# Folding two layer norms into neighbouring matmuls, splitting an inverse transform, and exponentiating one score bank ahead of its transposition

## The chip, the core and the metric

The kernel runs on one core of a Trainium2 chip. The metric is the device time of one execution in microseconds, less is better. The engines are named PE (TensorE, its weight loads shown as PEld), DVE (VectorE), ACT (ScalarE), POOL (GpSimd) and SP (SyncE, here a DMA queue).

## What is computed

One decoder layer on x of 16 x 64 x 128, with a layer norm ahead of each of three parts: self attention with 16 heads of 8 (whose reshape mixes positions and heads, so that a group of 64 rows attends to itself), an attention by circular correlation over FFTs, and a mixture of 8 experts of which each token takes 2.

```python
def _layernorm(x, axis=-1, eps=1e-05):
    m = jnp.mean(x, axis=axis, keepdims=True)
    v = jnp.var(x, axis=axis, keepdims=True)
    return (x - m) / jnp.sqrt(v + eps)
...
    x = x + _L0_attn_ref(_layernorm(x, axis=-1), L0_attn_Wqkv, ...)   # softmax(q k / sqrt(8)) v, then Wo
    x = x + _L0_xattn_ref(_layernorm(x, axis=-1), ctx_1024, ctx_1024, ...)
    x = x + _L0_ffn_ref(_layernorm(x, axis=-1), ...)
...
        corr = jnp.fft.irfft(jnp.fft.rfft(Q, axis=-1) * jnp.conj(jnp.fft.rfft(K, axis=-1)), n=Lv, axis=-1)
        top_vals, top_idx = jax.lax.top_k(corr, k_top)
        w = jax.nn.softmax(top_vals, axis=-1)
```

## The kernel before

The 1024 tokens are 8 tiles of 128, taken in 4 chunks of two tiles. Each piece of work is a step name.chunk.part, and `ORDER_TEXT` gives for every engine the order of its steps, written out in full; `BANK_TEXT` gives each PSUM result one of 8 banks. An engine takes its steps strictly in that order and waits in each for semaphores of the steps that it depends on, and PE also for the release of its bank by the step that held it last. There is no other scheduling, so a step that waits holds up all behind it on its engine.

Steps of a chunk, in order of dependence:

- Norm: st1 (statistics, DVE), rs1 (reciprocal deviation, two small operations on POOL, L308 and L310), nm1 (DVE, L467, two instructions: subtract the mean, multiply), xt (PE transposes xn, ACT copies it out).
- Attention: qkv (PE, then DVE adds the bias into `nat`, L481), vpar (POOL), ft (DVE, 32x32 transpositions, L492), vtr (PE and ACT), score (PE, L722, 32x64 pieces, into four banks of 128x512), then per bank smax (DVE, negated maximum of each head, L497), sub (DVE, adds it to the scores and writes one of three buffers of `low`, L503), pt (PE transposes `low`), exp (ACT, exponential out of PSUM into `prob`, L372); then pv (PE, L746; DVE normalises, L511 to L522), vt2, wo (PE; DVE adds to the residual `x12`, L528).
- Correlation: st2, rs2, nm2 (as above), dft (PE, forward transform of xn with the constant C_FWD), qp (PE; products with the keys' spectrum on DVE, L536 to L541), corr (PE, L785: three matmuls, each of 128 rows and 256 columns, into one bank), top (DVE, maxima and their places, L548 to L555), ex (ACT), w8 (DVE, six small parts), mix (POOL, L343), g, ov, y2 (PE, with copies on ACT; DVE adds y2 to `x12`). The context's transforms are cdft and cproj.
- Experts: st3, rs3, nm3, xt3, xtop (DVE, L597) and xsp (POOL) split the activation into two parts; gate and pick (DVE, eight small steps) choose the experts; wt (PE) turns the weights, SP stores them to DRAM and loads them back broadcast (wdma, L283 and L287) for rel. For each expert: up (PE, L834), rel (DVE, L641, scaled by the loaded weights), sq (ACT, L430), down (PE, L845, summed over experts); fin (DVE, L647) and store. up, rel, sq and down are numbered over the 32 pairs of chunk and expert. wtop, whi and wlo split the expert weights w_up (L602, L425, L328).

Each transposition or matmul in fp32 shows as two instructions in the trace. A warm-up of 12 matmuls opens PE's order. SP issues the loads; w_up (L278) is issued after all of x and the context have landed.

## Time and profile before

| | us |
|---|---|
| median of 3 runs | 143.54 (143.08 to 144.1) |
| the profiled execution's own time | 142.93 |
| its span from first to last instruction | 141.2 |
| PE busy | 123.0 (87%) |
| DVE busy | 104.1 (74%) |
| ACT busy | 54.9 (39%) |
| POOL busy | 38.5 (27%) |
| mean granted PE clock | 0.976 |

The span leaves 1.7 us of the profiled execution's time outside. Busy time is that of an engine's instructions; PE's are modelled at their ends. The shares are means over stages with different limits, so they are to be read by stretch.

### The profile page before, as it was taken

Reading aid. Unit: us, or ns where it says so; the run is one execution under the profiler, and the core shown is the slowest. Engines: PE = TensorE matmul, PEld = TensorE weight load, DVE = VectorE, ACT = ScalarE, POOL = GpSimd, SP = SyncE. Lnnn points to the kernel's source line nnn. Section 1 sums busy time; section 2 is a strip of 40 time slices with the busy share of each in tenths; the row PEclk is TensorE's granted clock in tenths of the full one; section 3 lists DMA queues with packets and bytes.
Section 4 is the critical chain, followed back from the end, with each engine's and each line's share of the span. In section 5 each row is a group of like instructions: output and inputs, shape, how many; then the busy total and the mean of one; then the engine's idle time right before and its main releaser. Section 6 shows DMA issues by size and latency. Waiting matters only on the chain.

```text
span 141.2 us, 4101 instructions
## 1 busy us (share of the span) xinstructions
PE 123.0 (87%) x1612; PEld 104.9 (74%) x1612; DVE 104.1 (74%) x341; ACT 54.9 (39%) x117; POOL 38.5 (27%) x71
## 2 busy tenths in 40 slices
PE   6749987856899998697899839999999999999992
PEld 2246556545788886585798836999989899999991
DVE  1349999999999879999797969836938664073711
ACT  2203354635517703172513034754325344170550
POOL 8579190460302020406663030411500300000000
PEclk9978999999999999999999986999999999999999
DMA  4888800000000000000000610610017172001001
GB/s 121 263 225 295 358 14 0 7 0 5 5 5 0 0 7 7 0 2 5 0 5 1 250 49 5 260 42 0 0 39 241 63 237 102 0 0 37 5 2 37
DMA packets 5027, 9.50 MB, mean 67 GB/s; under 512 B 368, under 2 KB 3856, under 8 KB 4240
## 3 DMA queue, kind: packets, MB, share of 16 engines
q1 hardware_dynamic: 4432, 8.50, 17.5%
q10 hardware_dynamic: 576, 0.73, 1.8%
q8 instruction: 13, 0.21, 0.6%
q14 instruction: 6, 0.05, 0.1%
HBM read 8.68 MB, written 0.56 MB: 65 GB/s over the span
## 4 chain that ended last, share of the span: by engine, by line
PE 51%; DVE 25%; issue 5%; DMA 4%; ACT 1%; POOL 1%; DVEq 0%
PE ps L845 21%; PE ps L834 14%; DVE negm L497 5%; DVE feat L492 4%; PE ps L785 4%; DVE low L503 3%; DMA wb_sb<-w_dram 3%; PE ps L821 2%; DVE nat L481 2%; DVE wtop L602 2%; PE ps L800 1%; DVE onat L511 1%; PE ps L792 1%; DVE topi L555 1%; PE ps L731 1%
## 5 line engine op out<-in xcount | busy, mean ns | idle before, releaser
L641 DVE SCALAR_TENSOR_TENSOR rel<-ps,wb_sb 128x512 f32<-128x512 f32 x32 | 21.8, 690 | 13.1 <-PE ps L834 7.2
L845 PE MATMUL ps<-wdn_sb,hid 128*128 128x128 f32 x256 | 30.6, 276 | 0.0
L430 ACT ACTIVATE hid<-rel 128x512 f32<-128x512 f32 x32 | 20.2, 631 | 25.1 <-DVE rel L641 16.9
L845 PEld LDWEIGHTS ps<-wdn_sb,hid 128*128 128x128 f32 x256 | 29.5, 192 | 0.3 <-issue 0.2
L834 PE MATMUL ps<-xhi,whi 128*128 128x256 f32 x64 | 19.2, 300 | 0.1
L834 PE MATMUL ps<-xhi,wlo 128*128 128x256 f32 x64 | 17.8, 278 | 0.0
L834 PE MATMUL ps<-xlo,whi 128*128 128x256 f32 x64 | 17.8, 278 | 0.0
L372 ACT ACTIVATE prob<-ps 128x512 f32<-128x512 f32 x16 | 9.1, 599 | 9.4 <-PE ps L731 9.4
L343 POOL TENSOR_TENSOR mix<-w,con 128x128 f32<-128x128 f32 x16 | 6.1, 412 | 23.3 <-DVE w L585 23.3
L834 PEld LDWEIGHTS ps<-xhi,whi 128*128 128x128 f32 x64 | 12.1, 189 | 0.5 <-issue 0.4
L834 PEld LDWEIGHTS ps<-xlo,whi 128*128 128x128 f32 x64 | 12.1, 189 | 0.0
L834 PEld LDWEIGHTS ps<-xhi,wlo 128*128 128x128 f32 x64 | 12.0, 188 | 0.0
L731 PE MATMUL ps<-con,low 128*128 128x128 f32 x64 | 9.3, 279 | 1.2 <-DVE low L503 1.1
L497 DVE TENSOR_REDUCE negm<-ps 128x8 f32<-128x512 f32 x16 | 10.3, 669 | 0.0
L503 DVE TENSOR_TENSOR low<-ps,negm 128x512 f32<-128x512 f32 x16 | 10.2, 673 | 0.0
L492 DVE STREAM_TRANSPOSE feat<-nat 128x512 f32<-128x512 f32 x16 | 10.0, 675 | 0.0
L785 PE MATMUL ps<-con,prod 128*128 128x256 f32 x24 | 7.0, 437 | 3.3 <-DVE rel L641 2.6
L722 PEld LDWEIGHTS ps<-feat 32*64 32x64 f32 x512 | 6.3, 130 | 4.7 <-issue 4.7
L722 PE MATMUL ps<-feat 32*64 32x64 f32 x512 | 7.3, 231 | 2.6 <-issue 1.5
L321 POOL TENSOR_TENSOR nat<-nat,con 128x256 f32<-128x256 f32 x8 | 5.1, 659 | 15.2 <-DVE nat L481 15.2
L310 POOL TENSOR_TENSOR rstd<-rstd,con 128x2 f32<-128x2 f32 x12 | 8.9, 745 | 1.0
L731 PEld LDWEIGHTS ps<-con,low 128*128 128x128 f32 x64 | 7.0, 141 | 3.0 <-DVE low L503 2.6
(103 smaller groups left out, 211.3 us busy)
## 6 DMA issues: line engine op xcount, KB each, us to landing
wb_sb<-w_dram SPq DMA_DIRECT2D x4, 1024.0 KB, 4.7
wup_sb<-w_up SPq DMA_DIRECT2D x1, 1024.0 KB, 6.0
wdn_sb<-w_down SPq DMA_DIRECT2D x1, 1024.0 KB, 8.0
c_sb<-ctxt SPq DMA_DIRECT2D x2, 256.0 KB, 6.8
out<-x_sb SPq DMA_DIRECT2D x4, 128.0 KB, 1.8
con<-consts SPq DMA_DIRECT2D x1, 400.0 KB, 3.0
wmid_sb<-w_mid ACTq DMA_DIRECT2D x1, 324.0 KB, 5.8
row_sb<-rows ACTq DMA_DIRECT2D x1, 260.0 KB, 4.9
```

Source lines behind the costliest of these rows:

```text
L310: nc.gpsimd.tensor_tensor(rstd[:, k, :], rstd[:, k, :], con[:, C_POW:C_POW + 2], ALU.pow).then_inc(done[name], 1)
L372: nc.scalar.activation(prob[:, a % 2, part].rearrange("p i t s -> p (i t s)"), psum("pt", a, part), ACT.Exp, scale=SCALE).then_inc(done["p ...
L430: nc.scalar.activation(hid[:, a % 3, :], rel[:, a % 2, :], ACT.Square).then_inc(done["sq"], 1)
L492: last = nc.vector.transpose(feat[:, c, a % 2, t].rearrange("p h (j r) -> p j h r", j=J), nat[:, t, c, :, :])
L497: nc.vector.tensor_reduce(negm[:, a, part, :], s_ps, AX.X, ALU.max, negate=True).then_inc(smax_ready, 1)
L503: nc.vector.tensor_tensor(low[:, step % 3].rearrange("p (h s) -> p h s", s=S), psum("score", a, part).rearrange("p (h s) -> p h s", s=S), ...
L641: nc.vector.scalar_tensor_tensor(rel[:, a % 2, :].rearrange("p (c t) -> p c t", c=2), psum("up", a).rearrange("p (c t) -> p c t", c=2), 0. ...
L722: last = mm(quads[r][S * g:S * (g + 1), S * h:S * (h + 1)], feat[32 * r:32 * r + 32, 0, a % 2, g, h, :], feat[32 * r:32 * r + 32, 1, a % 2 ...
L731: last = tr(t_ps[:, P * i:P * (i + 1)], low[:, step % 3, P * i:P * (i + 1)], ident)
L785: last = mm(c_ps[:, 0:NB * L], prod[:, a % 2, i, :], con[:, C_INV + NB * L * i:C_INV + NB * L * (i + 1)], start=(i == 0), stop=(i == 2))
L834: last = mm(z_ps[:, 2 * P * half:2 * P * (half + 1)], w[:, e, P * half:P * (half + 1)], r[:, c % 2, :], start=(i == 0), stop=(i == 2))
L845: last = mm(acc_ps[:, D * t:D * (t + 1)], hid[:, a % 3, 2 * P * half + P * t:2 * P * half + P * (t + 1)], wdn_sb[:, e, half, :], start=(e ...
```

## The change

- The norm ahead of qkv is folded. xt transposes raw x. The mean goes by centring the weights once: cent.0.0 (PE multiplies w_qkv by a matrix of 1/128, DVE subtracts the result from w_qkv) and cent.0.1 for the query weights of the second norm. The deviation goes into qkv's addition on DVE, now a scale and an add in one instruction. nm1 is gone.
- The norm ahead of dft is folded. dft reads `x12`; its deviation comes by fw: ACT scales the transform constant by it, two activations of 128 elements per chunk. nm2 is gone. `xn` shrinks to 4 tiles.
- The last of four score banks has no sub. DVE scales its negated maxima (negs, 128 x 8), and ACT takes exp(scale x score - maximum) out of the score bank head by head, 8 activations of 64 elements with a bias pointer (early), into a buffer of its own. PE transposes that, and ACT copies it to `prob` where it took exponentials. `low` has two buffers.
- corr is done in two halves: six matmuls of 64 rows and 128 columns, the two halves in different row halves of the array and in two banks.
- All orders but SP's and all banks are laid out anew.

The core of the diff; of the order texts, those lines that the text below speaks of.

```diff
     "PE": """
...
-        score.3.1 pt.2.3 vtr.3.1 pv.2.0 dft.1.0 pv.2.1 qp.1.0 pt.3.0 corr.1.0 g.0.0 pt.3.1 pt.3.2 pt.3.3 ov.0.0 pv.3.0 y2.0.0
-        vt2.2.0 pv.3.1 wo.2.0 g.1.0 ov.1.0 xt3.0.0 vt2.3.0 y2.1.0 gate.0.0 dft.2.0 wo.3.0 up.0.0 qp.2.0 up.1.0 up.2.0 xt3.1.0
-        up.3.0 corr.2.0 wt.0.0 dft.3.0 gate.1.0 up.4.0 qp.3.0 up.5.0 up.6.0 up.7.0 corr.3.0 wt.1.0 g.2.0 down.0.0 down.1.0
...
+        warm.12.0 xt.0.0 cent.0.0 cent.0.1 xt.1.0 qkv.0.0 qkv.0.1 xt.2.0 cdft.0.0 cdft.1.0 qkv.1.0 cproj.0.0 qkv.1.1 vtr.0.0
...
+        score.3.0 pt.2.3 score.3.1 vtr.3.1 pv.2.0 dft.1.0 pv.2.1 qp.1.0 pt.3.0 g.0.0 pt.3.1 corr.1.0 ov.0.0 pt.3.2 pt.3.3 y2.0.0
+        vt2.2.0 pv.3.0 pv.3.1 wo.2.0 xt3.0.0 vt2.3.0 gate.0.0 wo.3.0 g.1.0 dft.2.0 up.0.0 wt.0.0 qp.2.0 ov.1.0 dft.3.0 up.1.0
+        y2.1.0 qp.3.0 corr.2.0 up.2.0 up.3.0 corr.3.0 up.4.0 up.5.0 up.6.0 xt3.1.0 up.7.0 gate.1.0 g.2.0 down.0.0 ov.2.0 up.8.0
...
     "DVE": """
-        st1.0.0 nm1.0.0 st1.1.0 st1.2.0 nm1.1.0 st1.3.0 qkv.0.0 nm1.2.0 qkv.0.1 nm1.3.0 ft.0.0 ft.0.1 qkv.1.0 qkv.1.1 wtop.0.0
-        wtop.0.1 ft.1.0 ft.1.1 smax.0.0 smax.0.1 smax.0.2 sub.0.0 smax.0.3 sub.0.1 sub.0.2 sub.0.3 qkv.2.0 qkv.2.1 wtop.0.2
-        wtop.0.3 ft.2.0 ft.2.1 smax.1.0 smax.1.1 smax.1.2 smax.1.3 sub.1.0 sub.1.1 sub.1.2 pv.0.0 sub.1.3 pv.0.1 qkv.3.0 pv.0.2
-        qkv.3.1 ft.3.0 smax.2.0 smax.2.1 wo.0.0 smax.2.2 st2.0.0 smax.2.3 pv.1.0 sub.2.0 pv.1.1 nm2.0.0 pv.1.2 sub.2.1 sub.2.2
...
-        w8.1.3 w8.1.4 w8.1.5 y2.0.0 st3.0.0 pv.3.0 wo.2.0 pv.3.1 st2.2.0 nm3.0.0 pv.3.2 nm2.2.0 xtop.0.0 y2.1.0 st3.1.0 pick.0.0
-        wo.3.0 pick.0.1 st2.3.0 pick.0.2 nm3.1.0 pick.0.3 qp.2.0 pick.0.4 nm2.3.0 xtop.1.0 pick.0.5 pick.0.6 pick.0.7 top.2.0
-        top.2.1 pick.1.0 w8.2.0 pick.1.1 pick.1.2 w8.2.1 qp.3.0 w8.2.2 pick.1.3 w8.2.3 pick.1.4 w8.2.4 pick.1.5 w8.2.5 pick.1.6
-        pick.1.7 rel.0.0 rel.1.0 rel.2.0 rel.3.0 rel.4.0 top.3.0 top.3.1 w8.3.0 w8.3.1 w8.3.2 w8.3.3 w8.3.4 rel.5.0 w8.3.5
...
+        st1.0.0 cent.0.0 st1.1.0 cent.0.1 st1.2.0 qkv.0.0 st1.3.0 qkv.0.1 ft.0.0 ft.0.1 qkv.1.0 qkv.1.1 wtop.0.0 wtop.0.1 ft.1.0
+        ft.1.1 smax.0.0 smax.0.1 sub.0.0 sub.0.1 smax.0.2 smax.0.3 sub.0.2 negs.0.0 qkv.2.0 qkv.2.1 wtop.0.2 wtop.0.3 ft.2.0
+        ft.2.1 smax.1.0 smax.1.1 sub.1.0 pv.0.0 sub.1.1 pv.0.1 smax.1.2 pv.0.2 sub.1.2 smax.1.3 qkv.3.0 negs.1.0 ft.3.0 wo.0.0
...
+        top.0.0 wo.1.0 top.0.1 st2.1.0 w8.0.0 w8.0.1 w8.0.2 smax.3.0 w8.0.3 smax.3.1 w8.0.4 smax.3.2 w8.0.5 smax.3.3 sub.3.0
+        negs.3.0 sub.3.1 qp.1.0 sub.3.2 pv.2.0 top.1.0 pv.2.1 top.1.1 pv.2.2 w8.1.0 y2.0.0 w8.1.1 st3.0.0 w8.1.2 w8.1.3 pv.3.0
+        w8.1.4 pv.3.1 w8.1.5 nm3.0.0 pv.3.2 wo.2.0 st2.2.0 xtop.0.0 pick.0.0 pick.0.1 pick.0.2 wo.3.0 pick.0.3 st2.3.0 pick.0.4
+        pick.0.5 pick.0.6 pick.0.7 qp.2.0 y2.1.0 qp.3.0 top.2.0 st3.1.0 top.2.1 top.3.0 w8.2.0 top.3.1 w8.2.1 nm3.1.0 w8.2.2
+        w8.2.3 w8.2.4 w8.2.5 w8.3.0 w8.3.1 rel.0.0 w8.3.2 rel.1.0 w8.3.3 xtop.1.0 rel.2.0 w8.3.4 rel.3.0 w8.3.5 pick.1.0 rel.4.0
...
     "ACT": """
...
+        xt.0.0 xt.1.0 xt.2.0 cdft.0.0 cdft.1.0 cproj.0.0 vtr.0.0 whi.0.0 whi.0.1 vtr.0.1 vtr.1.0 cdft.2.0 vtr.1.1 xt.3.0 exp.0.0
+        cproj.1.0 exp.0.1 early.0.0 whi.0.2 whi.0.3 exp.0.2 exp.0.3 vtr.2.0 vtr.2.1 exp.1.0 vt2.0.0 exp.1.1 early.1.0 exp.1.2
+        exp.1.3 cproj.2.0 fw.0.0 vtr.3.0 exp.2.0 cdft.3.0 dft.0.0 exp.2.1 cproj.3.0 exp.2.2 vt2.1.0 early.2.0 ex.0.0 exp.2.3
+        vtr.3.1 fw.1.0 dft.1.0 early.3.0 g.0.0 exp.3.0 exp.3.1 ov.0.0 exp.3.2 exp.3.3 ex.1.0 vt2.2.0 xt3.0.0 vt2.3.0 gate.0.0
+        fw.2.0 g.1.0 dft.2.0 fw.3.0 wt.0.0 ov.1.0 dft.3.0 ex.2.0 ex.3.0 xt3.1.0 sq.0.0 sq.1.0 gate.1.0 g.2.0 sq.2.0 sq.3.0
...
     "POOL": """
...
-        vpar.2.0 vpar.2.1 wlo.0.2 wlo.0.3 vpar.3.0 vpar.3.1 rs2.0.0 rs2.1.0 mix.0.0 mix.1.0 rs3.0.0 rs2.2.0 xsp.0.0 rs3.1.0
-        rs2.3.0 xsp.1.0 mix.2.0 mix.3.0 rs3.2.0 xsp.2.0 rs3.3.0 xsp.3.0""",
+        rs1.0.0 x12.0.0 x12.1.0 rs1.1.0 x12.2.0 rs1.2.0 vpar.0.0 vpar.0.1 x12.3.0 rs1.3.0 vpar.1.0 vpar.1.1 wlo.0.0 wlo.0.1
+        vpar.2.0 vpar.2.1 wlo.0.2 wlo.0.3 vpar.3.0 rs2.0.0 vpar.3.1 rs2.1.0 mix.0.0 rs3.0.0 mix.1.0 rs2.2.0 xsp.0.0 rs2.3.0
+        rs3.1.0 mix.2.0 xsp.1.0 mix.3.0 rs3.2.0 xsp.2.0 rs3.3.0 xsp.3.0""",
...
+    if name == "corr":
+        return [(name, a, 0), (name, a, 1)]
...
-        xn = sb("xn", [P, TILES, D])
+        xn = sb("xn", [P, 4, D])
+        mean_of = sb("mean_of", [P, P])
+        fw = sb("fw", [P, 2, 2, 2 * 2 * NF])
...
-        low = sb("low", [P, 3, GROUPS * S])
+        low = sb("low", [P, 2, GROUPS * S])
+        early = sb("early", [P, GROUPS * S])
+        negs = sb("negs", [P, CHUNKS, GROUPS])
...
+                if name == "fw":
+                    act.wait_ge(done["rs2"], a + 1)
+                    if a == 0:
+                        act.wait_ge(ld_con, 16)
+                    if a >= 2:
+                        act.wait_ge(full["dft"], a - 1)
+                    for t in range(2):
+                        last = nc.scalar.activation(fw[:, a % 2, t], con[:, C_FWD:C_FWD + 2 * 2 * NF], ACT.Identity,
+                                                    scale=rstd[:, CHUNKS + a, t:t + 1])
+                    last.then_inc(fw_ready, 1)
...
+                if name == "early":
+                    act.wait_ge(negs_ready, a + 1)
+                    if a:
+                        act.wait_ge(turned, a)
+                    for h in range(GROUPS):
+                        last = nc.scalar.activation(early[:, S * h:S * (h + 1)], psum("score", a, QUAD - 1)[:, S * h:S * (h + 1)],
+                                                    ACT.Exp, bias=negs[:, a, h:h + 1], scale=SCALE)
+                    last.then_inc(early_ready, 1)
                 if name == "exp":
-                    act.wait_ge(full["pt"], QUAD * a + part + 1)
+                    if part == QUAD - 1:
+                        act.wait_ge(turned, a + 1)
+                    else:
+                        act.wait_ge(full["pt"], (QUAD - 1) * a + part + 1)
                     if a >= 2:
                         act.wait_ge(full["pv"], a - 1)
-                    nc.scalar.activation(prob[:, a % 2, part].rearrange("p i t s -> p (i t s)"), psum("pt", a, part), ACT.Exp,
-                                         scale=SCALE).then_inc(done["pt"], 1)
+                    if part == QUAD - 1:
+                        nc.scalar.copy(prob[:, a % 2, part].rearrange("p i t s -> p (i t s)"), psum("pt", a, part)).then_inc(done["pt"], 1)
+                    else:
+                        nc.scalar.activation(prob[:, a % 2, part].rearrange("p i t s -> p (i t s)"), psum("pt", a, part), ACT.Exp,
+                                             scale=SCALE).then_inc(done["pt"], 1)
...
+            nc.vector.memset(mean_of[:], 1.0 / D).then_inc(mean_ready, 1)
...
-                if name in ("nm1", "nm2", "nm3"):
-                    src = x_sb if name == "nm1" else x12
-                    k = CHUNKS * (int(name[2]) - 1) + a
-                    dve.wait_ge(stats_ready, LN_AT[("rs" + name[2], a)])
-                    dve.wait_ge(done["rs" + name[2]], a + 1)
-                    if name == "nm2":
-                        dve.wait_ge(full["xt"], a + 1)
-                    if name == "nm3":
-                        dve.wait_ge(full["dft"], a + 1)
-                    for t in range(2):
-                        last = nc.vector.tensor_scalar(xn[:, 2 * a + t, :], src[:, 2 * a + t, :], mv[:, k, t, 0:1], rstd[:, k, t:t + 1],
-                                                       ALU.subtract, ALU.mult)
+                if name == "nm3":
+                    k = 2 * CHUNKS + a
+                    dve.wait_ge(stats_ready, LN_AT[("rs3", a)])
+                    dve.wait_ge(done["rs3"], a + 1)
+                    if a >= 2:
+                        dve.wait_ge(full["xt3"], a - 1)
+                    for t in range(2):
+                        last = nc.vector.tensor_scalar(xn[:, 2 * (a % 2) + t, :], x12[:, 2 * a + t, :], mv[:, k, t, 0:1],
+                                                       rstd[:, k, t:t + 1], ALU.subtract, ALU.mult)
                     last.then_inc(done[name], 1)
+                if name == "cent":
+                    dve.wait_ge(full["cent"], part + 1)
+                    w = wmid_sb[:, W_Q:W_Q + D] if part else wqkv_sb[:]
+                    nc.vector.tensor_tensor(w, w, psum(name, 0, part)[:, 0:(D if part else 3 * D)], ALU.subtract).then_inc(done[name], 1)
...
+                    dve.wait_ge(done["rs1"], a + 1)
...
-                    nc.vector.tensor_tensor(nat[:, t, :, :, 32 - HD:32].rearrange("p c j d -> p (c j) d"), proj, bias,
-                                            ALU.add).then_inc(done["qkv"], 1)
+                    nc.vector.scalar_tensor_tensor(nat[:, t, :, :, 32 - HD:32].rearrange("p c j d -> p (c j) d"), proj,
+                                                   rstd[:, a, t:t + 1], bias, ALU.mult, ALU.add).then_inc(done["qkv"], 1)
...
+                if name == "negs":
+                    dve.wait_ge(smax_ready, QUAD * (a + 1))
+                    nc.vector.tensor_scalar(negs[:, a], negm[:, a, QUAD - 1], SCALE, None, ALU.mult).then_inc(negs_ready, 1)
                 if name == "sub":
-                    step = QUAD * a + part
-                    dve.wait_ge(smax_ready, step + 1)
-                    if step >= 3:
-                        dve.wait_ge(full["pt"], step - 2)
-                    nc.vector.tensor_tensor(low[:, step % 3].rearrange("p (h s) -> p h s", s=S),
+                    step = (QUAD - 1) * a + part
+                    dve.wait_ge(smax_ready, QUAD * a + part + 1)
+                    if step >= 2:
+                        dve.wait_ge(full["pt"], step - 1)
+                    nc.vector.tensor_tensor(low[:, step % 2].rearrange("p (h s) -> p h s", s=S),
                                             psum("score", a, part).rearrange("p (h s) -> p h s", s=S),
...
-                    corr = psum("corr", a)[:, 0:NB * L].rearrange("p (b s) -> p b s", s=L)
+                    corr = [psum("corr", a, b // 2)[:, L * (b % 2):L * (b % 2 + 1)] for b in range(NB)]
...
-                    dve.wait_ge(done["nm2"], a + 1)
+                    dve.wait_ge(full["dft"], a + 1)
...
-                    pe.wait_ge(low_ready, QUAD * a + part + 1)
+                    if part == QUAD - 1:
+                        pe.wait_ge(early_ready, a + 1)
+                    else:
+                        pe.wait_ge(low_ready, (QUAD - 1) * a + part + 1)
...
+                if name == "cent":
+                    if part == 0:
+                        pe.wait_ge(mean_ready, 1)
+                    pe.wait_ge(ld_mid if part else ld_wqkv, 16)
+                    w = wmid_sb[:, W_Q:W_Q + D] if part else wqkv_sb[:]
+                    mm(bank(name, 0, part)[:, 0:(D if part else 3 * D)], mean_of[:], w, start=True, stop=True).then_inc(full[name], 1)
                 if name in ("xt", "xt3"):
-                    if name == "xt" and a == 0:
-                        pe.wait_ge(ld_id, 16)
-                    pe.wait_ge(done["nm1" if name == "xt" else "nm3"], a + 1)
+                    if name == "xt":
+                        if a == 0:
+                            pe.wait_ge(ld_id, 16)
+                        pe.wait_ge((ld_x0, ld_x1, ld_x, ld_x)[a], 16)
+                    else:
+                        pe.wait_ge(done["nm3"], a + 1)
...
-                        last = tr(t_ps[:, P * t:P * (t + 1)], xn[:, 2 * a + t, :], ident)
+                        last = tr(t_ps[:, P * t:P * (t + 1)], x_sb[:, 2 * a + t, :] if name == "xt" else xn[:, 2 * (a % 2) + t, :], ident)
...
-                        pe.wait_ge(ld_wqkv, 16)
+                        pe.wait_ge(done["cent"], 1)
...
-                    step = QUAD * a + part
-                    pe.wait_ge(low_ready, step + 1)
+                    step = (QUAD - 1) * a + part
+                    if part == QUAD - 1:
+                        pe.wait_ge(early_ready, a + 1)
+                    else:
+                        pe.wait_ge(low_ready, step + 1)
                     t_ps = bank(name, a, part)
+                    source = early if part == QUAD - 1 else low[:, step % 2]
                     for i in range(PAIRS):
-                        last = tr(t_ps[:, P * i:P * (i + 1)], low[:, step % 3, P * i:P * (i + 1)], ident)
-                    last.then_inc(full[name], 1)
+                        last = tr(t_ps[:, P * i:P * (i + 1)], source[:, P * i:P * (i + 1)], ident)
+                    last.then_inc(turned if part == QUAD - 1 else full[name], 1)
...
-                    pe.wait_ge(done["nm2"], a + 1)
+                    pe.wait_ge(done["wo"], a + 1)
+                    pe.wait_ge(fw_ready, a + 1)
                     t_ps = bank(name, a)
                     spec = t_ps[:, 0:2 * P].rearrange("p (i t f) -> p i t f", i=2, t=2)
                     for t in range(2):
-                        last = mm(spec[:, :, t, :], xn[:, 2 * a + t, :],
-                                  con[:, C_FWD:C_FWD + 2 * 2 * NF].rearrange("p (i f) -> p i f", i=2), start=True, stop=True)
+                        last = mm(spec[:, :, t, :], x12[:, 2 * a + t, :], fw[:, a % 2, t].rearrange("p (i f) -> p i f", i=2),
+                                  start=True, stop=True)
...
+                    if a == 0:
+                        pe.wait_ge(done["cent"], 2)
...
-                    c_ps = bank(name, a)
+                    halves = [bank(name, a, two) for two in range(2)]
                     for i in range(3):
-                        last = mm(c_ps[:, 0:NB * L], prod[:, a % 2, i, :], con[:, C_INV + NB * L * i:C_INV + NB * L * (i + 1)],
-                                  start=(i == 0), stop=(i == 2))
+                        for two in range(2):
+                            rows = slice(2 * NF * two, 2 * NF * (two + 1))
+                            at = C_INV + NB * L * i + 2 * L * two
+                            last = mm(halves[two][:, 0:2 * L], prod[rows, a % 2, i, :], con[rows, at:at + 2 * L], start=(i == 0),
+                                      stop=(i == 2))
```

## Rows read from the trace of the kernel before

**Rows 1.** Windows of 10 us: window, length, busy time of each engine, clock, DMA.
```profile
10.00:20.00 10.00, 9.47 (x161) 6.17 (x159) 9.93 (x25) 4.33 (x8) 6.83 (x11) 0.90 0.67 249
...
20.00:30.00 10.00, 7.49 (x161) 5.66 (x162) 10.00 (x18) 5.44 (x10) 4.67 (x6) 1.00 0.01 2
...
40.00:50.00 10.00, 9.86 (x162) 8.74 (x161) 8.98 (x25) 6.07 (x14) 0.93 (x2) 1.00 0.02 4
...
60.00:70.00 10.00, 8.35 (x142) 6.92 (x140) 9.07 (x46) 5.30 (x18) 4.02 (x9) 1.00 0.01 2
...
80.00:90.00 10.00, 7.37 (x45) 5.68 (x44) 8.19 (x37) 4.09 (x8) 1.50 (x4) 0.83 0.22 88
...
100.00:110.00 10.00, 10.00 (x89) 9.62 (x88) 6.98 (x32) 3.94 (x8) 1.15 (x3) 1.00 0.34 116
```

**Rows 2.** Chain of work that ended last: start, length in us, what ran.
```profile
53.59 0.51 DVE xn L467 x2
...
74.58 1.29 PE ps L785 x6
...
78.16 4.24 DMA wb_sb<-w_dram
...
82.50 0.70 DVE rel L641
...
83.34 2.59 PE ps L785 x6
...
85.93 0.95 PE ps L821 x4
...
87.58 3.57 PE ps L845 x32
...
138.48 0.42 DVE x_sb L647
```

**Rows 3.** Timeline, four places: start, length, engine, line and operation.
```profile
10.37 0.34 SPq L278 DMA_DIRECT2D wup_sb<-w_up  x1
...
17.62 1.34 DVE L602 TENSOR_SCALAR wtop<-wup_sb 128x512 uint32<-128x512 uint32 x2
...
69.30 0.29 DVE L597 TENSOR_SCALAR xtop<-xn3T 128x256 uint32<-128x256 uint32 x1
...
70.84 0.36 PE L834 MATMUL ps<-xhi,whi 128*128 128x256 f32 x1
```

**Rows 4.** The page's DMA issues, w_up: count, size, us from issue to landing.
```profile
wup_sb<-w_up SPq DMA_DIRECT2D x1, 1024.0 KB, 6.0
```

**Rows 5.** Lines view, DVE: count, busy us, mean ns, idle before and releasers.
```profile
L503 DVE TENSOR_TENSOR low<-ps,negm 128x512 f32<-128x512 f32 x16 | 10.2, 673 | 0.0
...
L467 DVE TENSOR_SCALAR xn<-x,mv,rstd 128x128 f32<-128x128 f32 x16 | 4.7, 336 | 1.9 <-issue 1.9
...
L467 DVE TENSOR_SCALAR xn<-x_sb,mv,rstd 128x128 f32<-128x128 f32 x8 | 3.2, 443 | 1.2 <-POOL rstd L310 1.2
...
L560 DVE TENSOR_SCALAR topr<-topi 128x32 uint32<-128x32 uint32 x4 | 0.7, 164 | 0.0
...
L641 DVE SCALAR_TENSOR_TENSOR rel<-ps,wb_sb 128x512 f32<-128x512 f32 x32 | 21.8, 690 | 13.1 <-PE ps L834 7.2 <-ACT hid L430 4.4 <-DMA wb_sb<-w_dram 1.0
```

**Rows 6.** Lines view, ACT and POOL.
```profile
L385 ACT COPY valsT<-ps 128x64 f32<-128x64 f32 x16 | 2.2, 232 | 1.1 <-PE ps L754 1.0
...
L372 ACT ACTIVATE prob<-ps 128x512 f32<-128x512 f32 x16 | 9.1, 599 | 9.4 <-PE ps L731 9.4
...
L310 POOL TENSOR_TENSOR rstd<-rstd,con 128x2 f32<-128x2 f32 x12 | 8.9, 745 | 1.0
```

**Rows 7.** PE with small tiles: two pieces of the chain, one of the lines view.
```profile
48.45 0.84 PE ps L722 x53
...
96.22 0.61 PE ps L800 x16
...
L746 PE MATMUL ps<-prob,vkey 128*32 128x64 f32 x256 | 5.4, 222 | 0.6 <-issue 0.6
```

82 lines of the change are left out of this document (39 added, 43 removed).

## Prediction

> **What bounds the kernel now.** I read the windows first. From 10 to 60 us VectorE (DVE) is busy for 9 to 10 us of every ten, while TensorE (PE) has 7.5 to 9.9; from 90 us on PE is full and DVE is at 6 us or less of most tens. The hand-over lies in between: 60 to 70 has both near full, and in 80 to 90 PE stands still for 2.6 us at a granted clock of 0.83 [rows 1]. Then the chain of waits, in order of time: it runs almost wholly over DVE up to 44 us and again from 51 to 64, and from 69 us on over PE, with one detour: the expert weights of chunk 0 are stored and loaded back, rel.0 starts at 82.50, PE resumes at 83.34, and its first down is at 87.58. From there PE runs without a break to 138.46, where the last addition starts [rows 2]. So there are two terms to ask for: when DVE gets to xtop.0 (69.30 us, the last DVE step before the first up, whose matmuls start at 70.84 [rows 3]), and how long PE takes from there.
>
> The order texts make this clean: up to xtop.0 both kernels give DVE the same steps, but for eight nm1, nm2 and sub.3 kinds that go and the cent and negs steps that come. The tally of the set is exact; only its order changes.
>
> **Step A, the start.** The four nm1 go: 8 instructions, 3.2 us busy [rows 5], partly in gaps. cent.0 and cent.1 come: a subtraction of 384 and one of 128 elements. The forward pass qkv no longer waits for a normalised tile; its scale is folded into the addition, now a three-operand form. The form of L641 costs 690 ns for 512 elements and the plain addition of L503 673 [rows 5], so I price that at nothing. DVE would reach the first wtop about 2 us sooner than 17.62, but that step reads w_up, issued at 10.37 by SP behind the same waits as before [rows 3] and landing 6.0 us later [rows 4], at 16.4. So the gain is 17.6 - 16.4 = 1.2 us. SP's queue is untouched. On PE cent.1 stands ahead of xt.1 and qkv.0 and waits for w_mid; what is queued there is hidden as long as it delays qkv.0 by less than the 0.8 us that DVE would otherwise wait for w_up; beyond that the 1.2 shrinks, to 0 at worst. I take 1.2.
>
> **Step B, DVE from the first wtop to xtop.0.** This stretch was 69.30 - 17.62 = 51.7 us. Removed: four sub.3 at 10.2/16 = 0.64 us, 2.5 us; three nm2 (nm2.3 lies behind) of two instructions each, which took 0.51 us on the chain [rows 2] (4.7/16 = 0.29 apiece by the lines [rows 5], less overlap), 1.5 us. Added: four negs of 32 bytes a partition, like L560 at 164 ns [rows 5]; each follows its last smax and may wait a tenth, so 0.7 to 1.0, taken as 0.8. Sum: -3.2 us. low has two buffers where it had three: sub now waits for the transposition two steps back; two smax or another step stand between in each chunk, 0.6 us or more against a group of four matmul pairs of the same size, so I take nothing.
>
> **Step C, what ScalarE (ACT) takes over.** early: 8 activations of 64 elements from PSUM per chunk, 32 in all. The nearest row is L385, copies of 64 elements from PSUM: 232 ns each alone, 2.2/16 = 0.14 when overlapped [rows 6]. So one early is 1.1 to 1.9 us; I take 1.9, where a sub took 0.64. fw: two activations of 128 elements a chunk, 0.3 to 0.6 us. ACT is busy 6.1 us of the densest ten [rows 1], so this is load that fits; latency counts. The tightest chunk is 1: after negs.1 DVE has six passes over 512 elements a partition (two in ft.3.0, three smax, a sub) at L503's 0.64, and wo.0 and st2.0, some 1.2 together, so 5.0 us till it wants pv.1. Against that stand early 1.9, the transposition 0.5, exp.2 and the copy at 0.6 each [rows 6] and the pv matmuls, 5.4/4 = 1.35 less overlap [rows 7]: 4.6 to 5.0. So 0 to 0.4 us of cover; I add 0.5 us for this and its like. The bounds: 0, and 4 x 0.8 = 3.2 if all chunks are that tight and nothing overlaps.
>
> ScalarE has, by the Trainium skill's page "ScalarE: Activation LUTs", section "What ACT_TABLE_LOAD costs", 280 ns + 0.833 ns per element for an activation whose bias is a per-partition pointer, with some 93 ns overlapped: an estimate of 333 - 93 = 240 ns each, 1.9 us an early. L385 has no such pointer, so no run here shows it yet; it would leave the sum as it is.
>
> **Step D, from xtop.0 to the first down.** Before: 87.58 - 69.30 = 18.3 us, of which rel.0 starts at 82.50 - 69.30 = 13.2, with 1.0 of waiting for the wb load [rows 2, 5]. After, pick.0 is done first, so wt.0 comes early and the load (4.24 us for the way back alone [rows 2]) is off the path. In the DVE queue before rel.0, pick.1, xtop.1 and nm2.3 (13 instructions) are replaced by top.3 and the first of w8.3 (12), like for like: 12.2 us. But new waits appear. st2.2 now stands right before xtop.0, so on POOL rs2.2 (0.75 us [rows 6] and a small operation ahead of it, some 1.0) runs ahead of xsp.0, and dft.2, ahead of up.0 on PE, needs rs2.2 and then fw.2: up.0 starts 2.4 us after xtop.0, not 1.5. wt.0 then waits for the picks until 3.6. Behind it PE has qp.2 (result at 4.7; DVE is free at 3.4, idle 1.3), then ov.1, dft.3, up.1, y2.1 (result at 6.9; DVE free at 6.0, idle 0.9). So rel.0 starts at 12.2 + 2.2 = 14.4. g.2 and the first down follow rel.1, whose bank g.2 takes: 0.7 + 0.2 + 0.7 + 0.1 + a g of 0.5, at 16.7. Before, this took 5.1 us, since corr.3, wt.1 and g.2 came then at half clock (2.59 and 0.95 against 1.29 for the same corr [rows 2]). PE idles as long as before (xt3.1 waits for nm3.1, gate.1 for rel.0, some 3 us), but in pieces; I take full clock. D = 16.7 - 18.3 = -1.6 us.
>
> **The corr in halves** lies in this stretch for chunks 2 and 3. Before, 6 instructions take 1.29 us, 215 ns each. After, 12 of half the rows and half the columns. If pairs run side by side, 12 x 107/2 = 0.65; if not, 1.3. L722, 32-row pieces of 64 columns, goes at 0.84/64 = 13 ns each (the row counts 53 of a part's 64, some records are missing), where a full-height one of that width would take 54; L800, side by side in columns, at 0.61/16 = 38 [rows 7]. By the first 0.65, by the second 0.91; I take 0.8, with its entry and exit. That saves 0.5 a chunk. It is 2.0 us of PE over four chunks, but most goes into PE's idle time in this stretch; I count none beyond D.
>
> A rule speaks against it: the Trainium skill's "TensorEngine Tiling (Array Packing)", section "Key Properties", has TensorE drain on a change of tiling mode. In the chain L800's 16 pieces follow and precede full-height ones within 0.1 us [rows 7]; by the rule with a full drain at both ends the saving of 0.5 would be near nothing, by the row it stays.
>
> **Step E, behind the first down.** 138.46 - 87.58 = 50.9 us of unbroken PE. wt.1 now lies in it (+0.45); nothing else is added or removed. DVE and ACT have cover (PE 10.00, DVE 7 or less [rows 1]).
>
> **Sum.** -1.2 - 3.2 + 0.5 - 1.6 + 0.45 = -5.05 us: span 141.2 to 136.15. The profiled execution took 142.93, so 137.9; the median of the runs is 0.6 above it, 143.54, so 138.5.
>
> **Rivals.**
> Both waits go (0.13): DVE loses nothing in C and finds qp.2 and y2.1 ready, and PE's idle time before the first down falls away. -0.5 - 2.2 = 135.8, down to 134.5 with the corr saving in full. For it: the order was laid anew. Against: the queue positions above.
> Halves in series (0.10): corr stays at 1.3, 0.5 more for each of chunks 2 and 3: 139.5. L800 speaks for it, L722 against. By a rule of the skill's "TensorE: Matmul & The Clock Gate", section "LDWEIGHTS", a weight load goes by columns whatever its rows, so the halves load twice as much; the time it gives is this one.
> Given back at the hand-over (0.15): the waits of D double (+2.2) and PE's clock falls in them as at 83 us, (2.59 - 1.29) + 0.45 = 1.75 more: 142.5, no change. For it: PE stalls there in the kernel before too.
> Slower (0.10): early is slow on ACT, and DVE waits for pv in every chunk. It needs to eat 5.05 + 1.4 = 6.45 us, 1.6 a chunk; with cover 0.4, an early of 1.9 + 0.4 + 1.6 = 3.9 us, 0.49 per activation, twice L385. At 0.55 the time is 143.54 + 2 = 145.5.
>
> **How the numbers follow.** The forecast has 0.52 and its own range 137 to 140.5 (C from 0 to 1.5, A from 0.6 to 1.2). A measurement tells about 1% from no change, 1.4 us: faster is below 142.1. Faster: 0.52 + 0.13 + 0.10 and a little of the third rival, 0.77; same 0.13; slower 0.10. The range, leaving out the slower case, the top of the given-back one and the tail of the first rival, is 134.8 to 142.4.
>
> **What would show it.** Step A: first wtop (L602 before) at 16.4. B: xtop.0 at 65.4, DVE idle under 1 us between. C: 32 activations at about 0.23 in the lines view; ACT as releaser of DVE's pv if wrong. D: rel.0 14.4 and the first down 16.7 us behind xtop.0, granted clock 1.0 in between. Halves: 12 instructions in 0.8. E: 51.3 us of PE to the end. Most likely to be wrong: D, which hangs on queue positions rather than rows, and then C.

## The result, and the profile after

| | before | after |
|---|---|---|
| median of the runs, us | 143.74 (143.08 to 144.1) | 139.2 (137.75 to 139.81) |
| ratio to the kernel before | 1 | 0.9675, 95% interval 0.9586 to 0.9764 |
| profiled execution, its own time | 142.93 | 139.81 |
| its span, mean granted clock | 141.2, 0.976 | 138.0, 0.975 |

Ratios leave out runs over 1.5% above the shortest of the same kernel; medians are of all runs.

The change makes the kernel 3.2% faster, and 138.5 us had been forecast. Part of this agreement is luck. The prediction's sum gave the profiled execution a span of 136.15 us and a time of 137.9; they are 138.0 and 139.81, so 3.1 of the 5.05 us came. The median agrees because 0.6 us was added for a median above the profiled execution, and this time the profiled execution is the longest of four, 0.6 above the median. Inside the sum, terms were wrong in both directions: the start and VectorE's work shrank by more than counted, TensorE stood still in a place where nobody had looked, and the stretch behind the first down grew.

Line numbers of the kernel after: wtop L639, xtop L634, qkv L515, negs L534, sub L540, early L390, fw L374, score L773, pt L786, corr L846, up L895, wt L882, rel L678, down L906. The windows view, columns as in [rows 1]:

```profile
10.00:20.00 10.00, 9.37 (x178) 7.09 (x176) 9.93 (x23) 5.61 (x10) 8.15 (x12) 1.00 0.67 248
20.00:30.00 10.00, 6.81 (x155) 5.70 (x155) 9.81 (x18) 6.25 (x17) 4.01 (x4) 0.82 0.01 2
30.00:40.00 10.00, 9.05 (x224) 6.94 (x223) 6.22 (x14) 4.82 (x18) 0.61 (x1) 0.83 0.01 3
...
60.00:70.00 10.00, 6.99 (x106) 5.42 (x106) 8.41 (x44) 4.70 (x20) 5.46 (x12) 1.00 0.02 4
...
80.00:90.00 10.00, 9.24 (x84) 8.06 (x86) 8.90 (x33) 5.73 (x11) 4.91 (x12) 1.00 0.01 3
```

The kernel before had this between 30 and 40 us:

```profile
30.00:40.00 10.00, 7.89 (x255) 6.37 (x255) 10.00 (x20) 3.74 (x10) 1.89 (x3) 1.00 0.01 3
```

Against [rows 1], the hand-over (80 to 90) has lost its standstill and its low clock: PE 9.24 where it had 7.37. But between 20 and 40 us something new has come: the granted clock is 0.82 and 0.83, and in the second ten VectorE, the bound of this stretch, is busy only 6.22 us where it had 10.00. The timeline shows it, PE first, then the one DVE row with a long wait:

```profile
23.47 1.52 PE L773 MATMUL ps<-feat 32*64 32x64 f32 x121 [0.45 <-DVE low L540]
27.13 0.48 PE L773 MATMUL ps<-feat 32*64 32x64 f32 x7 [2.15 <-issue]
...
33.56 0.72 DVE L548 STREAM_TRANSPOSE onat<-ps 128x512 f32<-128x512 f32 x1 [3.75 <-PE ps L801]
```

Inside score.1.1 PE stops for 2.15 us, waiting for nothing that the profile shows, and the clock is at 0.50 (the 1.2 GHz level) from 27 to 33 us. The step pv.0 comes late and DVE stands 3.75 us. Then the hand-over and its end, the timeline again:

```profile
15.47 1.29 DVE L639 TENSOR_SCALAR wtop<-wup_sb 128x512 uint32<-128x512 uint32 x2
...
70.40 0.42 DVE L573 TENSOR_TENSOR prod<-ps,kv 128x256 f32<-128x256 f32 x1 [1.65 <-PE ps L833]
72.82 0.42 DVE L627 TENSOR_TENSOR x<-ps,x 128x256 f32<-128x256 f32 x1 [1.27 <-PE ps L868]
...
80.12 0.36 PE L895 MATMUL ps<-xhi,whi 128*128 128x256 f32 x1 [0.55 <-ACT xn3T L445]
81.44 0.58 PE L875 MATMUL ps<-wmid_sb,xn3T 128*128 128x8 f32 x4 [0.40 <-DVE rel L678]
82.84 1.13 PE L906 MATMUL ps<-wdn_sb,hid 128*128 128x128 f32 x8 [0.17 <-ACT eg L448]
```

xtop.0 starts at 65.77, rel.0 at 80.62 and the last addition at 135.36, so the 3.1 us by which that addition starts sooner are made of four parts:

| stretch | before | after | difference |
|---|---|---|---|
| to the first wtop | 17.62 | 15.47 | -2.15 |
| first wtop to xtop.0 | 51.68 | 50.30 | -1.38 |
| xtop.0 to first down | 18.28 | 17.07 | -1.21 |
| first down to the last addition | 50.90 | 52.52 | +1.62 |

The second row is what the experiments are about. Theory 1: it was to be -2.7 (B and C), and the standstill ate half of it. Theory 2: the early exponential on ScalarE is itself what makes pv.0 late. The two rivals of the prediction that the profile alone can't settle are also tested: what the halves of corr are worth, and where the hand-over's bound is.

### The profile page after: what moved, and what is told of

It reads as the page before. It is cut to its first block, busy times and chain, and to the rows that moved or that the text cites. A ratio compares the mean times of both kernels' runs of the same rounds, so it can differ in the third digit from the quotient of the medians.

```text
span 138.0 us, 4192 instructions
## 1 busy us (share of the span) xinstructions
PE 122.7 (89%) x1640; PEld 105.4 (76%) x1640; DVE 97.8 (71%) x328; ACT 63.9 (46%) x157; POOL 38.1 (28%) x71
## 4 chain that ended last, share of the span: by engine, by line
PE 53%; DVE 30%; issue 8%; DMA 5%; SPq 1%; ACT 0%; DVEq 0%
PE ps L906 20%; PE ps L895 14%; DMA x_sb<-x 5%; DVE feat L526 4%; DVE low L540 3%; DVE negm L531 3%; PE ps L801 3%; PE ps L786 3%; PE ps L773 2%; DVE rel L678 2%; DVE topi L592 2%; DVE nat L515 2%; PE ps L882 2%; DVE vals L557 1%; PE ps L743 1%
## 5 line engine op out<-in xcount | busy, mean ns | idle before, releaser
L678 DVE SCALAR_TENSOR_TENSOR rel<-ps,wb_sb 128x512 f32<-128x512 f32 x32 | 21.6, 684 | 13.9 <-ACT hid L461 9.8
L461 ACT ACTIVATE hid<-rel 128x512 f32<-128x512 f32 x32 | 20.2, 631 | 24.4 <-PE ps L906 14.0
L906 PE MATMUL ps<-wdn_sb,hid 128*128 128x128 f32 x256 | 31.0, 277 | 0.2 <-ACT eg L448 0.2
L906 PEld LDWEIGHTS ps<-wdn_sb,hid 128*128 128x128 f32 x256 | 29.5, 192 | 0.9 <-issue 0.8
L895 PE MATMUL ps<-xhi,whi 128*128 128x256 f32 x64 | 19.1, 298 | 0.7 <-ACT xn3T L445 0.6
L895 PE MATMUL ps<-xlo,whi 128*128 128x256 f32 x64 | 17.9, 279 | 0.0
L895 PE MATMUL ps<-xhi,wlo 128*128 128x256 f32 x64 | 17.9, 279 | 0.0
L895 PEld LDWEIGHTS ps<-xhi,whi 128*128 128x128 f32 x64 | 12.0, 188 | 1.5 <-issue 1.3
L895 PEld LDWEIGHTS ps<-xhi,wlo 128*128 128x128 f32 x64 | 12.0, 188 | 0.0
L895 PEld LDWEIGHTS ps<-xlo,whi 128*128 128x128 f32 x64 | 12.0, 188 | 0.0
L773 PE MATMUL ps<-feat 32*64 32x64 f32 x512 | 7.5, 232 | 3.4 <-issue 2.4
L773 PEld LDWEIGHTS ps<-feat 32*64 32x64 f32 x512 | 6.4, 131 | 5.1 <-issue 4.4
L315 POOL TENSOR_SCALAR rstd<-mv 128x2 f32<-128x2 f32 x12 | 2.7, 222 | 25.0 <-DVE mv L487 25.0
L403 ACT ACTIVATE prob<-ps 128x512 f32<-128x512 f32 x12 | 7.2, 615 | 3.7 <-PE ps L786 3.7
L786 PE MATMUL ps<-con,low 128*128 128x128 f32 x48 | 7.8, 290 | 0.8 <-DVE low L540 0.8
L540 DVE TENSOR_TENSOR low<-ps,negm 128x512 f32<-128x512 f32 x12 | 7.9, 665 | 0.0
L409 ACT COPY vkey<-ps 128x512 f32<-128x512 f32 x8 | 4.6, 586 | 6.3 <-PE ps L801 3.5
```

The source lines that it names most:

```text
L403: nc.scalar.activation(prob[:, a % 2, part].rearrange("p i t s -> p (i t s)"), psum("pt", a, part), ACT.Exp, scale=SCALE).then_inc(done["p ...
L461: nc.scalar.activation(hid[:, a % 3, :], rel[:, a % 2, :], ACT.Square).then_inc(done["sq"], 1)
L540: nc.vector.tensor_tensor(low[:, step % 2].rearrange("p (h s) -> p h s", s=S), psum("score", a, part).rearrange("p (h s) -> p h s", s=S), ...
L678: nc.vector.scalar_tensor_tensor(rel[:, a % 2, :].rearrange("p (c t) -> p c t", c=2), psum("up", a).rearrange("p (c t) -> p c t", c=2), 0. ...
L773: last = mm(quads[r][S * g:S * (g + 1), S * h:S * (h + 1)], feat[32 * r:32 * r + 32, 0, a % 2, g, h, :], feat[32 * r:32 * r + 32, 1, a % 2 ...
L786: last = tr(t_ps[:, P * i:P * (i + 1)], source[:, P * i:P * (i + 1)], ident)
```

## The experiments

All are compared with runs of the kernel before on the same chip. Those of each group also shared one chip: after_again, full_corr, sub_back and norm2_back; norm1_back, pt_first, fill and warm24; pt_first_again, rel_early, sub_pt and norm1_fair.

**The changed kernel once more**

> The changed kernel unaltered, as the yardstick for the partial ones on the same chip. Expected 139.2 us, some 0.97 of the kernel before. Its profile shows PE standing still for 2.15 us in the second score step (released by nothing the profile shows) and then half clock for about 7 us. If that belongs to the place in the instruction stream, it is there again at the same matmul; if it was an accident of one execution, it is gone or elsewhere.

139.6 us, ratio 0.9655 (0.9553 to 0.9757). The same place stalls again, for 1.88 us, and this time DVE waits 2.27 us for pv.0 and 0.78 for w_up at the first wtop:

```profile
16.52 0.76 DVE L639 TENSOR_SCALAR wtop<-wup_sb 128x512 uint32<-128x512 uint32 x2 [0.78 <-DMA wup_sb<-w_up]
...
27.38 0.34 PE L773 MATMUL ps<-feat 32*64 32x64 f32 x7 [1.88 <-issue]
```

So here w_up ends step A's gain, as predicted, 6.0 us after its issue. In the first execution it landed after 5.1 us, and DVE reached the first wtop at 15.47 without a wait.

**What the stall is: its place and what moves it**

Edits, against the changed kernel: in pt_first one PE step goes ahead of score.1.1; fill adds eight warm-up matmuls of 512 columns to that step; warm24 makes the warm-up of 24 matmuls of half the columns.

```diff
-        pt.0.1 score.1.0 score.1.1 pt.0.2 pt.0.3
+        pt.0.1 score.1.0 pt.0.2 score.1.1 pt.0.3
```

> One swap in PE's order: pt.0.2 goes ahead of score.1.1 (the second half of chunk 1's scores). Theory (the stall belongs to the place in PE's instruction stream, where new code is not there yet): it falls 4 matmuls earlier in score.1.1, after 57 to 59 of its 64 instead of 61, pt.0.2 and its exponential are no longer behind it, and the time falls by 0.3 to 1 us. Rival (the stall belongs to the score step itself): still before the last 3 to 7 pieces.

> As the swap above, and 8 matmuls of 512 columns on the warm-up's zeros, whose result is overwritten, stand in pt.0.2 before its transpositions. They take 1.7 us of PE where it would stand still. Theory: code arrives meanwhile, no stall or one of under 0.5 us is left in score.1.1, the granted clock stays at 1.0 from 27 to 34 us, DVE's idle time before pv.0 (3.75 us) is mostly gone, and the time falls by 1.5 to 3 us. Rival: the stall only moves behind the extra work and the time rises by up to 1.7 us.

> The warm-up has 24 matmuls of 256 columns instead of 12 of 512: same columns, 12 more matmuls in PE's stream. Theory of the place in the stream: the stall comes 12 matmuls earlier in score.1.1, after about 49 of 64. Rival (a time of its own, or the step itself): it stays before the last 3 to 7 pieces. Total time as the changed kernel's within 1 us.

PE's matmuls were counted from the start to the standstill, one window each. The kernel before:

```profile
0.00:29.90 29.90, 23.14 (x339) 14.70 (x340) 22.57 (x54) 11.43 (x20) 18.21 (x29) 0.94 0.47 151
```

The changed kernel, and then warm24:

```profile
0.00:26.50 26.50, 21.57 (x339) 14.14 (x340) 19.38 (x48) 12.85 (x28) 17.45 (x28) 1.00 0.55 171
```

```profile
0.00:26.50 26.50, 20.88 (x339) 15.44 (x340) 18.70 (x47) 12.64 (x28) 16.90 (x28) 1.00 0.54 171
```

339 matmuls in each, whichever steps those are (the same count in the other kernels with a stop, but 340 in norm1_back and norm1_fair). In pt_first the stop leaves 11 pieces of score.1.1 where 7 were left, 4 earlier, as the theory of the place had it (a transposition shows as one instruction, not two, so pt.0.2 counts 4); the expectation had only started from the wrong piece. Twelve more matmuls at the start make the stall come 12 pieces earlier (timeline of warm24: x109, then x19 after 2.19 us), and the kernel before has it too ("30.60 0.33 PE L722 ... x3 [1.46 <-issue]" in its timeline). So it is a place in PE's instruction stream, not a step. The DMA view says what comes shortly before: one packet of queue q8, of kind "instruction", 16 KB or a little more, here with a smaller one of q14 in the same slice (in the kernel before only that of q8 falls into such a window):

```profile
DMA  0000000000090000000000000000000000000000
GB/s 0 0 0 0 0 0 0 0 0 0 0 197 0 0 0 0 0 0 0 0 0 0 0 0 0 0 0 0 0 0 0 0 0 0 0 0 0 0 0 0
...
q8 instruction: 1, 0.02, 1.8%
q14 instruction: 1, 0.01, 0.5%
```

This is the window from 23 to 28 us in 40 slices, so the packet runs at 24.4 and PE goes on at 27.13, 2.7 us later. In the kernel before the packet is at 27.8 and PE goes on 2.8 later, in warm24 at 24.8 and 2.6 later, in norm1_back at 28.6 and 2.4 later, in rel_early at 25.1 and 2.2 later. In fill the packet is at 25.1. PE, held up by the eight long matmuls, reaches the place 45 pieces into score.1.1, at 27.6 or so, 2.5 us behind the packet, and runs through all 64 without a wait in the trace:

```profile
24.75 1.90 PE L786 MATMUL ps<-heat 128*128 128x512 bf16 x8
26.48 0.60 PE L788 MATMUL ps<-con,low 128*128 128x128 f32 x4
27.01 1.11 PE L772 MATMUL ps<-feat 32*64 32x64 f32 x64
```

The pieces of score take 12.6 ns each (1.52 us for 121), so the reading is that PE had used up the instructions it held before the next block could be used. It rests on the place, the time of the packet and fill; no run changed the supply itself. The Trainium skill's "Runtime: NRT & Kernel Launch", section "Instruction fetch mechanics", has instructions fetched in blocks of 16 KiB while the engine runs, mostly hidden; here they are not, by 1.0 to 2.2 us (0.98 in rel_early, 2.19 in warm24).

fill took 139.13 us (0.9683, 0.9599 to 0.9767) and pt_first 138.66 (0.9617, 0.9509 to 0.9725), their spans 136.1 and 136.0. That fill is no faster than pt_first, against the 1.5 to 3 us expected of it, doesn't price the stall: its long matmuls only fill the time that PE stands in pt_first, and the pieces of pv.0 start at 29.72 in the one and at 29.41 in the other. What the two share is pt.0.2 ahead of the place, so that ACT has exp.0.2 to do meanwhile and only pt.0.3 queues behind it; the clock stayed at 1.00 from 26 to 32 us in both. Both spans are 2 us shorter than the changed kernel's 138.0; in the medians less is left, 0.5 to 0.9 us for pt_first and 0.1 to 0.5 for fill. warm24, a single run, took 141.61 where the changed kernel's time within 1 us was expected, with 139.8 of span and clock 0.963.

**What the early exponential is worth**

Edit (sub_back): the fourth bank goes back to DVE and the common exponential; sub_pt is the same on top of pt_first.

```diff
-                    nc.vector.tensor_scalar(negs[:, a], negm[:, a, QUAD - 1], SCALE, None, ALU.mult).then_inc(negs_ready, 1)
+                    nc.vector.tensor_tensor(early[:].rearrange("p (h s) -> p h s", s=S),
+                                            psum("score", a, QUAD - 1).rearrange("p (h s) -> p h s", s=S),
+                                            negm[:, a, QUAD - 1, :].unsqueeze(2).broadcast_to([P, GROUPS, S]), ALU.add).then_inc(early_ready, 1)
```

> Undoes one part: the fourth score bank is again shifted on DVE, then turned, then exponentiated; the orders are kept, the subtraction stands where the scaling of the maxima (negs) stood. DVE gets 4 x (0.64 - 0.15) = 2.0 us more, ACT 7.0 us less. Theory: DVE is the limit up to xtop.0, so 2 us slower than the changed kernel. Rival: ACT's latency was costing what DVE gained, or DVE has idle time there (3.75 us in front of pv.0), so less than 0.7 us slower, or faster.

> The changed kernel with one step moved on PE: pt.0.2 from behind score.1.1 to ahead of it. It is the base of the two kernels run with it and is run again so that they can be set against it on one chip. Expected: 138.7 us as before (ratio to the kernel before 0.962); in the trace PE stands still 1.5 us inside score.1.1 after 53 of its 64 matmuls, no low clock from 27 to 34 us, xtop.0 at 63.1 us, first down at 80.8, and a second stretch of low clock at 63 to 67. If the low clock after the stall comes and goes from run to run, its times fall apart by about 2 us, between 137.7 and 139.8.

> The kernel pt_first_again with the early exponential taken back (sub.3 on DVE, four score banks treated alike). If moving the fourth bank to ACT is worth what the prediction gave it (DVE 2.5 us less, 0.8 for negs, 0.5 of waiting: 1.2 us), this one is 1.2 us slower than pt_first_again, once the stall that hid it in sub_back is out of the way: xtop.0 at 64.3 instead of 63.1. If it is worth nothing, because the eight short exponentials of one bank are as late for the transposition as sub.3 was, both are within 0.3 us. If the early exponential costs, xtop.0 comes before 63.0, as it did in sub_back (64.08 against 64.83).

sub_back: 140.16 us, 0.9782 (0.9689 to 0.9875), 0.6 above after_again, so its rival (less than 0.7) held and not the 2 us. pt_first_again: 138.37, 0.9668 (0.9618 to 0.9719). sub_pt: 139.55, 0.9727 (0.9672 to 0.9782), as expected. Four windows, each from the first wtop to xtop.0, columns as in [rows 1] (DVE's is the third busy time): the kernel before, the changed kernel, pt_first_again, sub_pt.

```profile
17.62:69.30 51.68, 42.92 (x999) 34.79 (x998) 49.55 (x146) 24.23 (x59) 16.08 (x26) 1.00 0.02 4
```

```profile
15.47:65.77 50.30, 41.66 (x935) 34.04 (x921) 45.94 (x140) 30.48 (x93) 14.79 (x24) 0.93 0.05 17
```

```profile
15.95:62.89 46.94, 38.79 (x898) 31.54 (x886) 45.84 (x138) 30.29 (x93) 14.25 (x23) 1.00 0.04 14
```

```profile
16.16:64.05 47.89, 39.38 (x922) 31.75 (x913) 47.55 (x138) 24.00 (x61) 14.38 (x24) 1.00 0.04 15
```

DVE's work falls by 3.6 us in both kernels with early (49.55 to 45.94 or 45.84); its idle time is 2.1 us before, 4.4 in the changed kernel and 1.1 with pt.0.2 moved. Early alone is the step from sub_pt to pt_first_again: 1.7 us less work, 0.28 us of new waiting for pv.0 and 0.36 for wo.0, and xtop.0 1.16 us sooner (0.95 counted from the first wtop); the medians are 1.2 apart, though the intervals overlap. In the order of the change that gain is not there: xtop.0 comes at 64.08 in sub_back and at 65.77 and 64.83 in the changed kernel. So neither the stall nor early costs much alone. In sub_back the same stall of 1.88 us is followed by no fall of the clock and no wait of DVE for pv.0. PE's steps behind the stall are the same in both, up to the pieces of pv.0 (first sub_back, then the changed kernel's pv.0):

```profile
27.33 0.34 PE L766 MATMUL ps<-feat 32*64 32x64 f32 x7 [1.88 <-issue]
...
29.71 1.10 PE L794 MATMUL ps<-prob,vkey 128*32 128x64 f32 x64
```

```profile
31.58 1.90 PE L801 MATMUL ps<-prob,vkey 128*32 128x64 f32 x64
```

From the end of the stall to the end of pv.0 that is 3.48 us at full clock, 6.35 in the changed kernel and 5.15 in after_again, in none of them with a wait of PE in between. An estimate from these rows: 2.9 of the 3.75 us that DVE waits, and 1.7 of the 2.27 in after_again, are the half clock; the remaining 0.6 to 0.9 is the stall, felt because DVE, with less work, comes to pv.0 sooner. PE did not wait there for early's result, ready at 25.3, so theory 2 holds only for the 0.28 and 0.36 us above. Whether early has a part in the fall of the clock stays open: sub_back is one trace.

**The halves of corr**

```diff
-                        for two in range(2):
-                            rows = slice(2 * NF * two, 2 * NF * (two + 1))
...
+                        last = mm(halves[0][:, 0:NB * L], prod[:, a % 2, i, :], con[:, C_INV + NB * L * i:C_INV + NB * L * (i + 1)],
+                                  start=(i == 0), stop=(i == 2))
```

> Undoes one part: corr again as three matmuls of 128 rows and 256 columns, in one bank, all else of the changed kernel kept. In the changed kernel the 12 halves took 0.87 to 0.89 us where the 6 full ones took 1.29, so 0.4 a chunk. Theory of the prediction (most of it goes into idle time of PE): within 0.5 us of the changed kernel. Rival (PE is the limit from chunk 0's corr on): 4 x 0.4 = 1.6 us slower.

141.91 us, 0.9878 (0.9788 to 0.9969); the span is 1.6 us longer than after_again's, the median 2.3, so the rival held. corr.0 starts 0.1 us later than in after_again, xtop.0 1.2 and the first down 1.6. The timelines, first of full_corr and then of the changed kernel:

```profile
48.46 0.63 DVE L585 MAX8 topv<-ps 128x8 f32<-128x64 f32 x4 [0.38 <-PE ps L843]
58.51 0.63 DVE L585 MAX8 topv<-ps 128x8 f32<-128x64 f32 x4 [0.45 <-PE ps L843]
...
74.00 1.46 PE L843 MATMUL ps<-con,prod 128*128 128x256 f32 x6
```

```profile
73.16 0.94 PE L846 MATMUL ps<-con,prod 64*128 64x128 f32 x12
```

Full corr takes 1.46 us a chunk, the halves 0.94. The prediction took 0.5 a chunk and counted none of it outside the hand-over. But in chunks 0 and 1 DVE waits for corr before its maxima, 0.38 and 0.45 us, and there are no such waits in after_again: a faster PE step is worth something in the stretch that DVE bounds, where DVE waits for that very step.

**Undoing the two folds**

> Undoes one part: nm2 is a DVE step again (two instructions a chunk, placed behind smax.2.2, smax.3.1, pick.0.2 and pick.0.7) and fw is gone from ACT. Theory: 3 to 4 x 0.51 us more on DVE, of which two lie ahead of xtop.0 and one delays wt.0: 1.0 to 1.5 us slower than the changed kernel. Rival: DVE's idle time at qp.2 and y2.1 takes it in: within 0.5 us.

142.25 us, 0.9824 (0.9731 to 0.9918), 2.7 above after_again where 1.0 to 1.5 were expected; its shortest run took 141.32. Its profile has 142.3 of span at a clock of 0.952, so it prices the fold only roughly. From the first wtop to xtop.0 it takes 50.82 us: 0.5 more than the changed kernel's first execution, whose stall (2.15) and wait for pv.0 (3.75 against 3.77) are alike, and 2.5 more than after_again, where 1.0 us was expected for two nm2.

> Undoes one part: nm1 is a DVE step again, xt transposes its result, the addition behind qkv is the plain one and the centring of w_qkv is gone; only the query weights are centred. Theory: DVE gets 8 instructions of 0.3 to 0.4 us in the first 14 us, so the first wtop starts some 2 us later (17.5 where the changed kernel had 15.47), and all behind it by as much: 1.5 to 2.1 us slower. Rival: the stall of PE in the second score step ends at a time of its own, so that the later start costs less than 0.7 us.

> The changed kernel with the first layer norm's fold undone (nm1 by DVE ahead of the transposition) and, unlike norm1_back, with the start of the kernel before: its order of nm1, st1 and qkv on DVE, cdft.0 ahead of qkv.0 on PE, and a place of its own for every nm1, so that nm1.3 waits for no transposition. Prediction step A: the fold is worth 1.2 us at the first wtop plus 1.9 less for qkv's scaling that comes back, so 1.2 to 2 us in all: 141.0. If norm1_back's 4.3 us were the fold's own worth, 143.5 here too. The first wtop tells: 17.6 us if the start of the kernel before is restored (norm1_back had 19.5). If PE standing from 6.4 to 8.3 brings the low clock of 8 to 12 us that the kernel before shows, PEclk reads 0.5 to 0.8 in that stretch again.

norm1_back: 143.84 us, 0.9943 (0.9885 to 1.0001). norm1_fair: 144.93, 0.9988 (0.9925 to 1.005). Their ratios lie 0.029 and 0.033 above after_again's, some 4 to 5 us, so both miss the 1.2 to 2.1 us expected, and neither measures the fold alone: the first wtop comes at 19.50 and 21.39, later than the 17.62 of the kernel before. POOL of norm1_back shows why, and DVE behind it:

```profile
13.30 0.61 POOL L328 TENSOR_TENSOR nat<-nat,con 128x256 f32<-128x256 f32 x1 [0.96 <-DVE nat L524]
13.88 0.73 POOL L321 TENSOR_TENSOR x<-x_sb,row_sb 128x256 f32<-128x256 f32 x1
14.57 0.22 POOL L315 TENSOR_SCALAR rstd<-mv 128x2 f32<-128x2 f32 x1
14.87 0.71 POOL L317 TENSOR_TENSOR rstd<-rstd,con 128x2 f32<-128x2 f32 x1
```

```profile
15.67 0.60 DVE L506 TENSOR_SCALAR xn<-x_sb,mv,rstd 128x128 f32<-128x128 f32 x2 [2.45 <-issue]
```

The change has put rs1.3 behind vpar.0 on POOL, which is harmless where the reciprocal deviation is wanted only after qkv. With nm1 back, DVE waits 2.45 us for it. norm1_fair, which mended PE's and DVE's order but not POOL's, has this wait too (2.46) and another of 3.19 for cent.1. Taking 2.45 off norm1_back's 19.50 gives 17.05, 0.5 to 1.6 us behind the changed kernel: what step A had. That is worked out, not measured, so what the first fold is worth stays open.

The same runs show a part of the fold that the prediction missed. The windows of 8 to 12 us, kernel before and then after:

```profile
8.00:10.00 2.00, 1.05 (x5) 1.08 (x6) 0.99 (x6) 0.00 (x0) 1.89 (x4) 0.64 0.74 174
10.00:12.00 2.00, 2.00 (x6) 1.37 (x5) 1.93 (x10) 0.59 (x1) 1.92 (x4) 0.50 0.81 228
```

```profile
8.00:10.00 2.00, 2.00 (x11) 1.42 (x12) 1.20 (x7) 0.37 (x1) 1.26 (x4) 1.00 0.79 178
10.00:12.00 2.00, 2.00 (x17) 1.74 (x16) 1.93 (x9) 1.44 (x3) 1.92 (x4) 1.00 1.00 255
```

Before, PE stands from 6.5 to 8.95 us and then works at half clock until 12. The fold gives it cent.0, cent.1 and a transposition of raw x in that gap, and the clock stays full. With nm1 back the low clock is back (0.64 and 0.50 in norm1_fair).

**The hand-over in another order**

Edit, on top of pt_first, DVE's order and then PE's, cut to the steps that move (on ACT gate.1 also goes ahead of sq.1):

```diff
-  top.3.0 w8.2.0 top.3.1 w8.2.1 nm3.1.0 w8.2.2 w8.2.3 w8.2.4 w8.2.5 w8.3.0 w8.3.1 rel.0.0 w8.3.2 rel.1.0
+  top.3.0 top.3.1 nm3.1.0 rel.0.0 w8.2.0 w8.2.1 w8.2.2 rel.1.0 w8.2.3 w8.2.4 w8.2.5 rel.2.0 w8.3.0 w8.3.1
...
-  gate.1.0 g.2.0 down.0.0 ov.2.0 up.8.0 down.1.0 g.3.0
+  gate.1.0 down.0.0 down.1.0 g.2.0 ov.2.0 up.8.0 g.3.0
```

> The kernel pt_first_again with the hand-over in another order: on DVE top.3.1, nm3.1 and rel.0 ahead of w8.2, on PE down.0 and down.1 ahead of g.2, on ACT gate.1 ahead of sq.1. Theory (the hand-over is held by DVE's order, as prediction step D has it: rel.0 is not late because the broadcast of the gates is late): rel.0 goes from 78.6 to 76.4 us and the first down from 80.8 to 78.5, and since PE has 1.1 us of idle pieces there (0.55 for xt3.1, 0.38 for rel.0, 0.17 for gate.1), the end comes 0.8 to 1.1 us earlier: 137.7. Rival (PE's work is the bound there already, and what it gains now it stands later for g.2, whose mix.2 is 0.7 us later, or for y2.2): within 0.3 us of pt_first_again. Rival (the broadcast lands at 74 us or later and PE has nothing ready): slower.

140.39 us, 0.9747 (0.9675 to 0.9819), 2 us slower than pt_first_again by the medians. rel.0 starts at 77.54 against 77.74, the first down at 80.64 against 79.96, and PE then waits for the steps that were pushed back:

```profile
80.64 2.02 PE L903 MATMUL ps<-wdn_sb,hid 128*128 128x128 f32 x16 [0.36 <-ACT eg L445]
83.77 0.69 PE L858 MATMUL ps<-mixT,kv 128*64 128x64 f32 x16 [0.68 <-ACT mixT L430]
```

The expectation fell for two reasons. This execution had a low clock in the hand-over (0.83 from 60 to 80 us), and DVE waited 2.99 us for qp.2, 1.65 in pt_first_again, so the 2.2 us that the order should have given were mostly used up: xtop.0 to the first down took 17.83 us against 17.07. And PE met the steps that were pushed back at a worse time: ov.2, now right behind g.2, waits 0.68 us for ACT's copy of g.2's result, and wt.1 waits 0.80 us for the delayed pick.1. This is the larger part: from the first down to the last addition it is 54.62 us against 52.52, of which 0.6 is g.2, now behind the first down, and 1.48 the two waits.

**One program, with and without low clock.** The kernels of pt_first and pt_first_again are the same. Their profiled executions have clocks 0.987 and 1.000, spans 136.0 and 135.1, and first downs at 80.82 and 79.96. From xtop.0 to the first down:

| execution | clock in the hand-over | us |
|---|---|---|
| after | 1.00 from 60 to 88 | 17.07 |
| pt_first_again | 1.00 from 60 to 88 | 17.07 |
| pt_first | 0.57, 0.50, 0.50, 0.72 in the ones from 63 to 67 | 17.73 |
| after_again | 0.84, 0.50, 0.81 in the twos from 64 to 70 | 17.96 |
| sub_back | 0.77, 0.50, 0.50, 0.52 in the twos from 62 to 70 | 18.80 |

So a stretch of low clock there costs 0.7 to 0.9 us in one program (1.7 in sub_back, against the changed kernel), and it comes in some executions and not in others. Such stretches can account for the spread of the changed kernel's runs: 139.81 and 139.63 us at a mean clock of 0.975, 138.77 and 137.75 at 0.988 and 0.987. They are why the moves above are seen better in stretches of a profile than in medians.

## Why the prediction was right, point by point

- **Step A, -1.2: the mechanism right, the size too small here.** w_up bounds it in after_again, as the 0.78 us of waiting shows, and not in the first execution. It was issued at 10.3 to 10.5, much as before, but landed within 5.1 to 6.0 us, so the gain was 1.1 to 2.15. What it did not see is PE's clock from 8 to 12 us.
- **Step B, -3.2: too small, and its waits left out.** DVE has 3.6 us less work in this stretch. negs took 156 ns each, so 0.6 with no wait, where 0.8 was taken; nm2 and sub.3 were near their price. qkv in its three-operand form, priced at nothing by the two 512-element forms in [rows 5], takes 603 ns for 384 elements by the lines view where the addition took 532: 0.07 apiece, 0.3 us over the four in this stretch. These parts come to 3.1, so 0.5 of the 3.6 us is not assigned. The sum also counted only work: DVE's 2.1 us of waiting before (0.94 for wo.1 and 0.66 ahead of nm2.2, part of the 1.9 "issue" of L467 in [rows 5]) fell to 0.4 in sub_back, in the change's own order, and the prediction had no term for that.
- **Step C, +0.5: the price right, the place and the real cost wrong.** An early is 1.75 us against 1.9, 219 ns per activation (32 in 7.0 us). The estimate of 240 ns that the prediction worked out from the Trainium skill's "ScalarE: Activation LUTs", section "What ACT_TABLE_LOAD costs", agrees within a tenth. The waits that early brings are 0.64 us, in chunk 0 and not in 1. The cost in the changed kernel, 3.75 + 0.22 us, came from the stall ahead of that transposition and, for 2.9 of it, from the half clock that followed. The failed step is that only latencies of steps were summed, with PE's queue taken as free and its clock as full: the kernel before shows the same standstill, 1.46 us, in which DVE did not wait, and the prediction passed over it. xtop.0 came at 65.77, near the 65.4 forecast, only because A and B had given more; that is luck.
- **Step D, -1.6: right but for 0.4.** Measured -1.2, 17.07 against 16.7; rel.0 14.85 behind xtop.0 against 14.4; DVE idle 1.65 and 1.27 at the two places named, against 1.3 and 0.9; PE waits 0.55, 0.40 and 0.17; clock 1.00. The forecast of full clock held in this execution and not in after_again, so of the rival "given back at the hand-over" the low clock is real, for 0.9 us where it had 1.75; the doubled waits are not (DVE 2.42 and 1.26 in after_again).
- **The halves, 0.8 a chunk and nothing beyond D: the price near, the conclusion wrong.** 0.94 by the timeline against 1.46, 0.5 saved as assumed, so they run side by side; by its own estimate of 0.65 at most 0.3 is left for entry, exit and what the Trainium skill's "TensorEngine Tiling (Array Packing)", section "Key Properties", says of draining, which no run here shows by itself. But they are worth some 1.5 us in the span, 0.8 of it as DVE waits for corr.0 and corr.1. The rival "halves in series" is out.
- **Step E, +0.45: too small, +1.6 measured.** In the lines view behind the first down wt has 12 matmuls and 1.8 us where it had 8 and 1.2 (0.6), down 31.0 us where it had 30.6 (0.4), and PE is idle 0.1 us between 85 and 90. About 0.5 us is not assigned. It belongs to the order and not to one execution: the eleven other traces with this order have 52.51 or 52.52 us here. So the assumption that only wt.1 is added there failed.
- **The range** held, but it is wider than its terms: C from 0 to 1.5 and A from 0.6 to 1.2 give 138.0 to 140.1, not 137 to 140.5. A slip on which nothing rests: at 0.55 us an activation the slow case is 146.9 by its own terms, not 145.5. The rival "slower by early" is out: an activation of 64 elements would have had to take 0.49 us.

## What to carry to other kernels

When a step is moved from one engine to another, add to its own latency whatever stands ahead of its consumer in the consumer's queue, stalls "for issue" included: a standstill that costs nothing before the change is the first place to look for its bill. A step that a bound engine waits for is worth its saving even if its own engine has time to spare. An edit that loosens a dependence also loosens the orders around it, so a part can't be undone alone without giving back the order on every engine, POOL's too.

## What the hardware showed

- Many tiny matmuls in a row seem to outrun the supply of instructions: among 12.6 ns pieces PE stopped for 1.0 to 2.2 us ahead of its 340th matmul (341st in norm1_back and norm1_fair) in every kernel but fill, and resumed 2.2 to 2.8 us after the packet of instructions. 1.9 us of long matmuls ahead of the place hid it.
- The clock after such a stop isn't settled by its length: after 1.88 us it fell to 0.50 in after_again and norm1_back and stayed at 1.00 in sub_back. It fell in all five traces with a stop of 2.15 or 2.19 us and in none of the five with 0.98 to 1.53. What decides was not found. It can cost more than the stop: 2.9 us behind the one of 2.15.
- Two matmuls of 64 rows on two halves of the array overlap: one after the other the 12 would take 1.3 us by the prediction's rate, and they took 0.94, 78 ns for a piece of 64 rows and 128 columns with its share of entry and exit (0.94/12), against 243 for one of 128 rows and 256 columns (1.46/6).
